# Cross-attention and mixture of experts: first block's maxima in two stages, Wq and Wk multiplied on chip, four blocks of two tiles

## The reference

```
h  = layernorm(x)
q  = h @ Wq + bq ;  k = ctx @ Wk + bk ;  v = ctx @ Wv + bv
x  = x + tanh(g_xattn) * (softmax(q k^T / sqrt(128)) @ v)
h  = layernorm(x)
r  = softmax(h @ Wr + br), two largest of 8 kept and divided by their sum
y  = sum over e of r[e] * (relu(h @ W1[e] + b1[e]) @ W2[e] + b2[e])
out = x + tanh(g_ffn) * y
```

## Time and profile before

| | us |
|---|---|
| median of 3 runs (lowest, highest) | 304.34 (303.92, 305.04) |
| profiled execution | 305.22 |
| its span, first to last instruction | 303.10 |
| first scores of block 0 | 33.18 |
| first scores of block 1 | 80.05 |
| first matmul of the experts | 203.65 |
| mean granted TensorE clock | 0.989 |

### The profile page before, as it was taken

How to read it: one execution, slowest core, us unless ns; L and a number is a source line. 1 busy time by engine, 2 the same in 40 slices (tenths; PEclk the granted TensorE clock), 3 DMA queues, 4 the chain that set the end, 5 groups by cost and what they waited for, 6 DMA issues and landing times.

```text
span 303.1 us, 4501 instructions
## 1 busy us (share of the span) xinstructions
PE 289.5 (96%) x1577; PEld 252.3 (83%) x1577; DVE 220.0 (73%) x395; ACT 211.3 (70%) x333; POOL 81.7 (27%) x81
## 2 busy tenths in 40 slices
PE   6798899999999999999999989899999999999995
PEld 5565699999999999998999979888878878888883
DVE  4589699998598987995347478855868956756666
ACT  2678656666575665657677757669879889888881
POOL 5999940000000300000002944433141311111310
PEclk9889799999999999999999999999999999999999
DMA  7500400000000000000000252221011121121120
GB/s 209 211 0 3 138 1 3 0 2 0 2 0 2 1 0 2 0 0 4 0 0 2 69 139 71 73 67 71 32 39 35 41 68 35 42 99 36 37 67 35
DMA packets 10641, 12.40 MB, mean 41 GB/s; under 512 B 1530, under 2 KB 6524, under 8 KB 10620
## 3 DMA queue, kind: packets, MB, share of 16 engines
q1 hardware_dynamic: 10140, 11.90, 12.9%
q10 hardware_dynamic: 480, 0.23, 0.3%
HBM read 11.57 MB, written 0.56 MB: 40 GB/s over the span
## 4 chain that ended last, share of the span: by engine, by line
PE 87%; DVE 7%; POOL 2%; issue 2%; ACT 1%; DMA 1%; DVEq 0%; POOLq 0%; ACTq 0%
PE ps L872 8%; PE ps L873 8%; PE ps L893 8%; PE ps L808 8%; PE ps L874 8%; PE ps L895 8%; PE ps L894 8%; PE ps L939 5%; PE ps L941 5%; PE ps L940 5%; PE ps L967 4%; PE ps L968 4%; PE ps L966 4%; DVE pmax L584 3%; POOL norm L361 1%
## 5 line engine op out<-in xcount | busy, mean ns | idle before, releaser
L532 ACT ACTIVATE ex_hi<-ps 128x768 fp32r<-128x768 f32 (+1 forms) x78 | 57.0, 731 | 62.7 <-PE ps L874 62.1
L697 DVE TENSOR_TENSOR ex_lo<-ps,ex_hi 128x768 fp32r<-128x768 f32 (+1 forms) x78 | 66.4, 852 | 29.0 <-ACT ps L533 27.4
L584 DVE TENSOR_REDUCE pmax<-ps 128x1 f32<-128x512 f32 (+1 forms) x104 | 65.8, 666 | 11.5 <-PE ps L808 10.3
L738 DVE TENSOR_TENSOR ex_lo<-ps,ex_hi 128x512 fp32r<-128x512 f32 x64 | 44.0, 691 | 29.8 <-ACT ps L548 29.2
L533 ACT ACTIVATE ps<-ps 128x768 f32<-128x768 f32 (+1 forms) x78 | 56.5, 724 | 0.0
L872 PE MATMUL ps<-q_hi,ctxT_hi 97*128 97x384 f32 (+1 forms) x153 | 50.1, 327 | 2.9 <-DVE ex_lo L697 2.4
L547 ACT ACTIVATE ex_hi<-ps,cols 128x512 fp32r<-128x512 f32 x64 | 44.2, 691 | 11.6 <-PE ps L941 10.8
L893 PE MATMUL ps<-ex_hi,ctx_hi 128*97 128x384 f32 (+1 forms) x153 | 49.6, 324 | 0.0
L873 PE MATMUL ps<-q_lo,ctxT_hi 96*128 96x384 f32 (+1 forms) x153 | 49.5, 324 | 0.0
L874 PE MATMUL ps<-q_hi,ctxT_lo 96*128 96x384 f32 (+1 forms) x153 | 49.1, 321 | 0.0
L895 PE MATMUL ps<-ex_lo,ctx_hi 128*97 128x384 f32 (+1 forms) x153 | 48.7, 318 | 0.0
(11 more groups left out here) (117 smaller groups left out, 443.8 us busy)
## 6 DMA issues: line engine op xcount, KB each, us to landing
w_raw<-in_L_ffn_W_dram SPq DMA_DIRECT2D x16, 256.0 KB, 3.1
r_b<-routing SPq DMA_DIRECT2D x16, 256.0 KB, 3.2
raw<-in_ctx_dram SPq DMA_DIRECT2D x6, 384.0 KB, 6.1
tok<-in_x_dram SPq DMA_DIRECT2D x1, 384.0 KB, 4.3
out_dram<-norm SPq DMA_DIRECT2D x1, 256.0 KB, 2.5
tok<-in_x_dram SPq DMA_DIRECT2D x1, 128.0 KB, 2.3
out_dram<-norm SPq DMA_DIRECT2D x1, 128.0 KB, 1.7
out_dram<-norm ACTq DMA_DIRECT2D x1, 128.0 KB, 1.8
```

The source lines that it names most:

```text
L532: nc.scalar.activation(ex_pair(ex_hi, u % P_RING, js, n), scores, ACT.Exp)
L584: nc.vector.tensor_reduce(pmax[:, FIRST_TILE[b] + t, place:place + 1], MPAIR[:, s % 2, 0:w], AX.X, ALU.max).then_inc(max_reduced, 1)
L697: nc.vector.tensor_tensor(ex_pair(ex_lo, u % P_RING, js, n), whole, ex_pair(ex_hi, u % P_RING, js, n).bitcast(F32), ALU.subtract).then_inc ...
```

## The change

- The blocks are four of two tiles.
- Block 0's maximum is taken in two stages. The first takes the first 24 chunks (six windows, 12 slots) and goes into the row of `q_hi`. Units 0 to 11 use it. Meanwhile the other 14 slots run in units 1 to 7, and the maximum over all keys goes into the row of a second copy, `q_two`, used by units 12 to 25. Their value sums are gathered in another bank.
- The sums of units 0 to 11 are projected by themselves (unit 16), scaled by exp of the difference of the two rows (`shift_step`, two one-column matmuls), and added to the projected sums of the later units at the gate.
- Wq and Wk^T are multiplied on chip (`mq_sb`), with the bias as a row. A query then takes one matmul from the turned tokens, and one with a single contraction row for the bias.
- The context is transposed in windows of four chunks: six ahead of block 0, seven in its units 0 to 6, with their copies on ScalarE. The queries of blocks 2 and 3 are made in units 7 to 10 of block 0.
- Block 0's tokens are normalized on VectorE instead of POOL. POOL's splits stand in a written-out order with the normalizations of blocks 1 to 3.
- There are 25 or 26 slots for the maxima of a later block in each block before: block 1's in units 0 and 9 to 21, the others' in units 0 to 21. `P_RING` is 4.

VectorE in the start, before: all 26 reductions (L584) stand ahead of the addition to the row (L595).

The diff, cut to its core:

```diff
-BLOCK_TILES = [2, 3, 3]
+BLOCK_TILES = [2, 2, 2, 2]
 NB = len(BLOCK_TILES)
 FIRST_TILE = [sum(BLOCK_TILES[:b]) for b in range(NB)]
 SPANS = 2
-TRANSPOSE_GROUP = 8
+NATURAL_GROUP = 8
+WINDOW = 4
+FIRST_WINDOWS = 6
 LAG = 2
-P_RING = 3
+P_RING = 4
...
+    SLOTS = window_slots(0, range(FIRST_WINDOWS))
+    START_SLOTS = len(SLOTS)
+    SLOTS_AT = {}
+    STAGE_DONE = {}
+
+    def place_slots(v, slots):
+        SLOTS_AT[v] = range(len(SLOTS), len(SLOTS) + len(slots))
+        SLOTS.extend(slots)
+
+    second = window_slots(0, range(FIRST_WINDOWS, NW))
+    ahead = window_slots(1, range(NW))
+    place_slots(0, ahead[0:2])
+    for k in range(NW - FIRST_WINDOWS):
+        place_slots(1 + k, second[2 * k:2 * k + 2])
+    SECOND_MAX_UNIT = NW - FIRST_WINDOWS
+    STAGE_DONE[1] = len(SLOTS)
+    SECOND_ROW_UNIT = SECOND_MAX_UNIT + 1
+    assert SECOND_ROW_UNIT < FIRST_UNITS
+    MAX_UNIT = UNITS - 5
+    ROW_UNIT = UNITS - 4
+    left, places = ahead[2:], range(SECOND_ROW_UNIT + 1, MAX_UNIT + 1)
+    for k, v in enumerate(places):
+        place_slots(v, left[k * len(left) // len(places):(k + 1) * len(left) // len(places)])
+    STAGE_DONE[2] = len(SLOTS)
+    for b in range(1, NB - 1):
+        left, places = window_slots(b + 1, range(NW)), range(0, MAX_UNIT + 1)
+        for k, v in enumerate(places):
+            place_slots(b * UNITS + v, left[k * len(left) // len(places):(k + 1) * len(left) // len(places)])
+        STAGE_DONE[b + 2] = len(SLOTS)
+    STAGE_DONE[0] = START_SLOTS
...
+        LATER_TURN = {2: NW - FIRST_WINDOWS, 3: NW - FIRST_WINDOWS + 2}
+        ROWS_UNIT = NW - FIRST_WINDOWS + 4
+        assert ROWS_UNIT < FIRST_UNITS
+        SPLIT_SLOT = [3, 9]
+        NATURAL_UNIT = {2: 2, 3: 6, 4: 9, 5: 11, 6: 13}
+        EARLY_COPY, EARLY_PROJECT, EARLY_SCALE = FIRST_UNITS + 2, FIRST_UNITS + 3, FIRST_UNITS + 4
+        assert set(NATURAL_UNIT) == set(range(2, NG))
+
+
+        MAX_AT = {1: SECOND_MAX_UNIT, 2: MAX_UNIT, 3: UNITS + MAX_UNIT, 4: 2 * UNITS + MAX_UNIT}
+        ROW_AT = {1: SECOND_ROW_UNIT, 2: ROW_UNIT, 3: UNITS + ROW_UNIT, 4: 2 * UNITS + ROW_UNIT}
+        FIRST_OF_STAGE = {0: 0, FIRST_UNITS: 1, UNITS: 2, 2 * UNITS: 3, 3 * UNITS: 4}
...
+            nc.scalar.copy(wkqT[:, :], UB[1][:, 0:CA + P]).then_inc(small_copied, 1)
+            act.wait_ge(fold_made, 1)
+            nc.scalar.copy(mq_sb[:, :], UB[1][:, CA + P:2 * CA + P])
+            nc.scalar.copy(bias_row[:, :], UB[1][0:1, 2 * CA + P:3 * CA + P]).then_inc(fold_copied, 1)
...
+            copy_ctxT_hi(1)
+            copy_ctxT_whole(0)
...
+            def beside_first_block(i):
+                w = FIRST_WINDOWS + i
+                if w < NW:
+                    copy_ctxT_hi(w)
+                    copy_ctxT_whole(w)
+                for b, unit in LATER_TURN.items():
+                    if i == unit:
+                        copy_x(b)
+                    if i == unit + 1:
+                        copy_qk(b)
+                if i == ROWS_UNIT:
+                    act.wait_ge(rows_turned, 1)
+                    nc.scalar.copy(cols[:, :], UB[0][:, 0:NROW]).then_inc(rows_copied, 1)
+                    nc.scalar.activation(tanh_g[:, :], gates[:, :], ACT.Tanh).then_inc(tanh_ready, 1)
+                for g, unit in NATURAL_UNIT.items():
+                    if i == unit:
+                        copy_ctx(g)
+                if i == EARLY_COPY:
+                    act.wait_ge(ex_used, FIRST_UNITS)
+                    nc.scalar.copy(early_u[:, :], UB[1][0:CA, 0:width(0)]).then_inc(early_copied, 1)
+                if i == EARLY_SCALE:
+                    nt = BLOCK_TILES[0]
+                    act.wait_ge(early_made, 1)
+                    nc.scalar.activation(early_scale[:, :], UB[1][:, nt * (HID + 1):nt * (HID + 2)],
+                                         ACT.Exp).then_inc(early_scaled, 1)
+                    act.wait_ge(early_scaled, 1)
+                    for t in range(nt):
+                        last = nc.scalar.activation(early[:, t, :], UB[1][:, t * (HID + 1):(t + 1) * (HID + 1)],
+                                                    ACT.Copy, scale=early_scale[:, t:t + 1])
+                    last.then_inc(early_done, 1)
...
+            def row_max(m):
+
+                b = stage_block(m)
+                row = q_two[C:CA, :] if m == 1 else q_hi[C:CA, span(b)]
+                dve.wait_ge(max_row, m + 1)
+                nc.vector.tensor_tensor(row, MPAIR[C:CA, 0, 0:width(b)], row.bitcast(F32), ALU.add).then_inc(row_ready, 1)
+                if m == 1:
+                    dve.wait_ge(row_ready, 2)
+                    nc.vector.tensor_tensor(shift_step[C:CA, :], q_two[C:CA, :].bitcast(F32),
+                                            q_hi[C:CA, span(0)].bitcast(F32), ALU.subtract).then_inc(step_ready, 1)
...
+            dve.wait_ge(rstd_ready, 1)
+            for t in range(BLOCK_TILES[0]):
+                last = nc.vector.tensor_scalar(norm[:, t, :], tok[:, t, :], mv[:, 0, t, 0:1], rstd[:, 0, t:t + 1],
+                                               ALU.subtract, ALU.mult)
+            last.then_inc(first_norm, 1)
             dve.wait_ge(x_later_in, 16)
-            for b in range(1, NB):
-                statistics(0, b)
-            for s in range(len(SLOTS[0])):
-                reduce_max(0, s)
-                for b in range(NB):
+            statistics(0, 1)
...
+                    if b == 0:
+                        dve.wait_ge(early_done, 1)
+                        step(nc.vector.tensor_tensor(proj, proj, early[:, :, :], ALU.add))
...
+            nc.tensor.transpose(UB[1][:, CA:CA + P], wq_sb[:, :], ident[:, :]).then_inc(small_turned, 1)
+            pe.wait_ge(small_copied, 1)
+            nc.tensor.matmul(UB[1][:, CA + P:2 * CA + P], wqT, wkT, start=True, stop=True)
+            nc.tensor.matmul(UB[1][0:1, 2 * CA + P:3 * CA + P], bq_sb[:, :], wkT, start=True, stop=True).then_inc(fold_made, 1)
...
+            def turn_window(w):
+
+                js = window_chunks(w)
+                bank = ps[:, w % 4, :] if w < FIRST_WINDOWS else UB[0]
+                pe.wait_ge(ctx_in[js[0] // NATURAL_GROUP], 16 if js[-1] < FULL else 32)
+                if w >= FIRST_WINDOWS:
+                    pe.wait_ge(x_copied, 2)
+                    pe.wait_ge(ctxT_f_ready, w)
+                elif w >= 4:
+                    pe.wait_ge(ctxT_f_ready, w - 3)
+                for k, j in enumerate(js):
+                    last = nc.tensor.transpose(bank[0:C, k * P:(k + 1) * P], raw[:, j, :], ident[:, :])
+                last.then_inc(ctx_turned, 1)
...
+            def make_qk(b):
+                dst = qk_home(b)[0:CA, :]
+                pe.wait_ge(fold_copied, 1)
+                pe.wait_ge(row_ones, 1)
+                if b:
+                    pe.wait_ge(q_lo_ready, b)
+                if b >= 2:
+                    pe.wait_ge(x_copied, b + 1)
+                nc.tensor.matmul(dst, bias_row[:, :], ones_row[:, 0:width(b)], start=True, stop=False)
                 pe.wait_ge(x_copied, b + 1)
-                nc.tensor.matmul(UB[1][:, 0:width(b)], wq_sb[:, :], xT[:, span(b)], start=True, stop=True).then_inc(q_made, 1)
-
-            def make_qk(b):
-                pe.wait_ge(q_copied, b + 1)
-                nc.tensor.matmul(UB[0][0:CA, 0:width(b)], wkT[:, :], qT[:, 0:width(b)], start=True,
-                                 stop=True).then_inc(qk_made, 1)
-
-            def score_for_max(b, s):
-                t, key, w, place = SLOTS[b][s]
+                nc.tensor.matmul(dst, mq_sb[:, :], xT[:, span(b)], start=False, stop=True).then_inc(qk_made, 1)
...
+            turn_window(0)
             make_qk(0)
-            turn_ctx(1, 0, TRANSPOSE_GROUP)
-            pe.wait_ge(q_hi_ready, 1)
-            per_group = TRANSPOSE_GROUP * P // BANK * BLOCK_TILES[0]
-            TURNED = [0, 0, 0, 4, TRANSPOSE_GROUP]
-            assert per_group == len(TURNED) - 1
-
-            def query_steps(g):
-                for b in range(1, NB):
-                    if Q_STEPS[b, "turn"] == g:
+            turn_window(1)
+            turn_window(2)
+            turn_window(3)
+            for s in range(START_SLOTS):
+                score_for_max(s)
+                if s == 3:
+                    turn_x(0, 1, UB[0])
+                    turn_window(4)
+                if s == 5:
+                    make_qk(1)
+                    turn_window(5)
+            turn_max(0)
...
+                first = q_two[:, :] if b == 0 and i >= FIRST_UNITS else q_hi[:, span(b)]
```

371 lines of the change are left out of this document (217 added, 154 removed).

## The result

The changed kernel took 323.95 us (median of four: 320.68, 323.93, 323.97, 324.46) against 304.69 for the kernel before beside it (303.92 to 309.35): a ratio of 1.0596, 95% interval 1.0535 to 1.0658. The ratios leave out single runs that a slow state of the chip lengthened; medians and ranges hold all runs. Forecast were 310.3 us and 302.5 to 316.0. The direction was right, the size was not, and the time lies outside the range. The profiled execution took 324.46 us with a span of 322.5.

What follows compares the result with a forecast made beforehand. TensorE, busy 96%, was taken as the bound, with time to save only in the start. -11.1 + 7.95 + 2.6 - 2.5 + 9.3 = +6.25: span 303.1 to 309.35, hence 310.3 us after adjustments; range 302.5 to 316.

Steps and rivals of the forecast that it cites:

- The start: Before the first scores: first reduction at 10.4 us, 12 maxima instead of 26, first scores at 22.1 against 33.18, -11.1 us.
- a sign of being wrong: Start: the prediction called itself wrong if the start was not under 24 us.
- What comes back behind the start: TensorE work from the loose start now lies where TensorE is full: +7.95 us, queries and bias rows +1.7 of it.
- Four blocks of two tiles: Attention blocks: 2.88 us per chunk instead of 2.83, times 51 chunks, +2.6 us (+1.9 at 0.119 a column block).
- The weight ring: Last block: expert 2's weights land late, so VectorE and then the scores wait 3.6 us.
- Rival D: Last block: the 3.6 us hole brings the clock down again, at a cost of 1.7 us; 312 us, chance 0.12.
- Four fifths: Attention blocks: new waits counted at 11.6 us, cut to 9.3 because the count gave 2.2 for a measured 1.49.
- Rule on ports: Start: VectorE's new tensor_scalar and POOL's fill shut each other out, perhaps a microsecond; 311.4 instead of 310.3.
- Rival C: First block bound by ScalarE: 0.6 us in each of seven units, +4.2 instead of 1.5; 313 us, chance 0.08.
- A: Faster: start at 20.6 us, blocks absorb follow-up steps, waits 3.5 instead of 9.3; 303.3 or 302.6 us, chance 0.16.
- B: No change: start at 21.3 us, waits of 5.2; 305 us, chance 0.19.

Runs made afterwards that it cites:

- a_late: The changed kernel with the query steps of blocks 2 and 3 and the bias rows moved to units 18 to 22 of the first block: 319.86 us.
- a_pool_order: The kernel of a_pool with the maxima's matmuls before, not behind, the extra steps in each unit of the first block: 313.03 us.
- a_again: The changed kernel run once more with no edit: 319.93 us, ratio 1.044.
- a_pool: The changed kernel with POOL splitting expert 0's weights before it normalizes the third block's tokens: 314.38 us, ratio 1.0225.
- a_slack: The kernel of a_pool with one more small fill on VectorE before the remainder in every unit of the last block: 317.93 us.
- a_fill: The changed kernel with 32 unread transposes on TensorE in the last block, before the scores that wait for expert 2's weights: 318.0 us.
- a_busy: The changed kernel with three more transposes in the start, behind the transposition of Wq: 320.84 us.
- a_memset: The changed kernel with POOL's long fill of ctxT_hi put ahead of its first inverse deviation: 320.46 us.

## Why the prediction was right in its direction and wrong in its size

Against the profile with the quicker start (span 318.0; forecast 309.35) 8.65 us are missing: first scores -0.7, first block +5.6, middle blocks +1.4 (92.42 against 91, twice the middle of 45 to 46), last block +4.0 (47.53 against 43.5), experts -0.5; these make 9.8, since the forecast's stage lengths, rounded as they were, add up to 1.2 less than its span. The first result lies another 4.5 us above: 3.4 in the start, 0.6 in the first block and 0.5 in the last. The forecast had no term for a second course of the start.

- *The start.* Right in the shorter course: 10.52 for 10.4, 21.44 for 22.1. The twelve reductions took 9.1 us for 10.3, and the way from the last of them to the scores 1.8 for 1.4, at a clock that had fallen at 19.0 us. The 24.85 of the first profile is the same work with matmuls at half pace until 16 us. It is later than the 24 that the prediction named as a sign of being wrong, and than the 23.6 of its range.
- *What comes back behind the start.* The first step that failed. The queries of blocks 2 and 3 and the bias rows stood there at 1.7 us, "from such matmuls of 128 to 256 columns"; a_late measures 4.1 to 4.5. A one-row matmul of 256 columns costs 0.60, no less than a full one, and TensorE waits for q_lo before it may turn the next tokens. That is 2.6 of the first block's 5.6; 1.6 of the steps' cost is the wait of the reductions behind them (a_pool_order, units 9 and 11): the forecast added durations where it should have followed who stands behind whom. The other 3.0 were not taken apart by an experiment, and their cause stays open. The profile shows unit 22, in which the second block's maxima become a row, at 2.51 us for 1.67 in unit 21; unit 15, with the early projection, at 2.83 for 1.89, where 0.6 was forecast; and units 0 to 6 at 17.9 together in a_again, partly at the low clock, and 17.5 in a_pool.
- *Four blocks of two tiles.* The middle blocks were 1.4 us too long together, which was not followed. The units at width 256 are 1.43 to 1.44 us where nothing lies beside them, and that the round trip has no slack over the block is shown by a_slack. By its own figures the term is 2.45 us (0.048 x 51) and not 2.6, and the lower value about 1.5 at most and not 1.9; that changes little.
- *The weight ring.* The mechanism was right in each of its numbers, but the hole's price was not its own length. This is the second step that failed. Rival D, which held that the clock falls again, was no alternative to the forecast: it was its consequence, and should have stood in the sum, which had nothing for it. It had a chance of 0.12 and a price of 1.7 us; a_fill measures 2.4. That is 2.4 of the last block's 4.0. The rest is not the hole's: a_pool, with neither hole nor low clock, has 42.13, where the forecast less its hole (3.6, as cut to 2.9) has 40.6.
- *Four fifths.* The count of waits was 11.6 us and was cut to 9.3, because the same count had come out too high for one wait of the kernel before. Whether that was a mistake is not shown. These are the windows of a_again's four blocks (length, then busy time of TensorE and the other columns as above):

```profile
21.44:80.06 58.62, 56.08 (x393) 50.58 (x394) 45.34 (x83) 40.23 (x81) 23.90 (x24) 0.96 0.07 19
80.06:126.38 46.32, 45.55 (x349) 42.52 (x349) 38.44 (x80) 28.47 (x55) 2.31 (x3) 1.00 0.01 1
126.38:172.48 46.10, 45.42 (x349) 42.54 (x349) 38.11 (x79) 29.29 (x58) 2.30 (x3) 1.00 0.01 1
172.48:220.01 47.53, 42.14 (x318) 40.65 (x319) 27.93 (x65) 29.13 (x58) 20.33 (x17) 0.93 0.22 67
```

  TensorE's idle time in them adds up to 9.4 us, near the 9.3 as cut. But its busy time holds each matmul's way through the pipeline, which hides short waits, so this is no clean count either.
- *Rule on ports.* The trace agrees for the new pair (1.55 against 0.60) in that VectorE stands; the 1 us that it would have added to the sum was not there, because the product of Wq and Wk was as late.
- *Rival C* (a first block bound by ScalarE, 0.6 a unit in units 0 to 6) did not happen: units 3 to 6 take 2.32 to 2.44 us, TensorE's own 2.26 and a little. *A* and *B* would have needed waits of under 4 and of 5.2 us, against 9.4 us of idle time.

## What to carry to other kernels

Price a wait of TensorE of the hole's length (3.5 us here) with what its clock takes afterwards, and look first at whether it can be filled or its cause reordered on an engine that is "not the bottleneck". Count steps inserted in a pipelined loop by the round trip they lengthen, not by their own durations. And run the changed kernel once more as it is beside the experiments: without it, two edits to the start (a_busy, a_memset) would each have been credited with 3 us, and a_pool with 4 us too many.

## What the runs showed of the hardware that was not expected

- The same program has more than one course of its start: first reduction at 14.34 or at 10.52 us, with the matmuls at half pace until 16 us in the first, while the granted clock is recorded as 1.00. The kernel before scatters as well, from 302.2 us of span at a mean granted clock of 0.994 to 307.3 at 0.972; only one of its runs has a trace, so whether its start does it is not shown.
- A matmul with one contraction row and 256 columns held TensorE 0.60 us until the next began; one with 128 rows held it 0.32 and 0.61.
- 3.5 us of idle TensorE brought 6.8 us at a granted clock of 0.50 (0.52 in the window of the first profile); 32 transposes in its place brought 1.00, and the kernel's median fell by 1.9 us (319.93 to 318.0) with more work.
- A fill of 1536 columns in one partition on POOL took VectorE's two normalizing instructions from 0.60 to 1.55 us; the fill itself was not slowed (1.37 and 1.38).
